# A block of attention and quantised FFN on one core: a normalisation's root begun by ScalarE, and context's split moved to the end of a step's first half

## Chip, cores and metric

The kernel runs on one NeuronCore of a Trainium2 chip. The metric is device time in microseconds, from a run of the program to its end. Lower is better.

## What is computed

The input x is 16 x 256 x 512 in fp32, the context has the same shape. The reference, cut to what matters:

```python
x = x + xattn(layernorm(x), ctx, ctx, wq, wk, wv, wo_w, wo_b)   # 16 heads of 32, rope, window 128
x = x + ffn(layernorm(x), W_in, b_in, W_out, b_out)             # 8-bit weights, 16-bit activations, gelu

def _layernorm(x, axis=-1, eps=1e-05):
    m = jnp.mean(x, axis=axis, keepdims=True)
    v = jnp.var(x, axis=axis, keepdims=True)
    return (x - m) / jnp.sqrt(v + eps)
```

The change concerns the first layernorm (its 1/sqrt(v + eps)), the order of work in the attention part, and one PSUM bank.

## The kernel before

The program is written engine by engine, each with its own instruction list in a fixed order; semaphores are the only coupling. Three parts follow each other: attention over 16 sequences (0 to some 760 us), the first FFN product, the second. Nothing in the second and third part is touched.

**The attention part** has a prologue and 16 steps, one for each sequence b. Step b does three things at a time: the scores, softmax and weighted sum of sequence b; the projections of sequence b + 1 (`has_proj`); the output product, residual and second normalisation's moments of sequence b - 1 (`has_o`). It also prepares sequence b + 2 (`has_xt`): its context is split, and the first normalisation's factors are found.

fp32 products are made of three fp32r products: each operand is split into a `_hi` (ScalarE, a cast) and a `_lo` (the difference, by VectorE or GpSimd).

A step has two halves.

- In the first half, TensorE makes the scores of 16 heads (`scores`, L605), and between them the tiles of b + 1: k (L521 to L523), the transpositions of x (`x_transposes`, L534), v, q. VectorE takes each head's row maxima (`row_maxima`, L1192), and between them `invert(b - 1)` (the reciprocal of the softmax sums, L1233), the rest of x, the rotations of k, and `normalise(b - 1)` (L1239).
- In the second half, TensorE makes the scores again, transposed (`scores_t`, L639), ScalarE their exponentials (`softmax_exp`, L961), GpSimd cuts them to the window (`band`, L1529), and TensorE multiplies them in four groups of four heads (`clump`: weighted sums L653, softmax sums L666). Among them stand the 24 products of `o_products` (L589) for b - 1, and before the last group `w_transposes` (L687), which needs a column block of W_in that VectorE has quantised.

**Around the change.**

- `ln1(j)` on VectorE: bn_stats and bn_aggr of two halves, then the root of v + eps by the bit trick and three Newton steps (`rsqrt_seed`, `rsqrt`, L285 to L293), then nmr = -mean x rstd. Seventeen linked instructions; each waits for the one before by the semaphore `ln1_chain`. `norm1(j)` on ScalarE applies it to x.
- `ctx_hi(j)` on ScalarE (L912, one cast of 128x1024) and `ctx_lo(j, quarter)` on GpSimd (L1512, four quarters of 128x256) split the context. `ctx_hi` waits for the load and for the v tiles of j - 1, which read the same buffer.
- `x_transposes(j, s)` writes half s to `q_bank[s]`, banks 4 and 5. Bank 5 also holds the softmax sums, so half 1 waits for `den_done`, the end of L1233.
- `oT_copy` (L931) brings the weighted sums out of banks 6 and 7; `centre` (L949) makes x minus its mean, whose largest magnitude VectorE then takes (`largest`, L1163).
- SyncE issues every transfer, in one order. In a step: load x for the residual of b - 1 (L325), store the reciprocals (`den_scratch`, L356), wait, load them back spread out (the "shares", L359), load x of b + 2, spread the maxima (L350), then the stackings of k and q of b + 1 (`stack_group`, L343; a group's first waits for `k_lo` or `q_lo`), the next block of W_in, the next context, more stackings, and the store of b - 1 (L329). The load L325 waits for that store. `normalise` needs the shares.

Of the kernel before, what the change touches and what calls it, by code (L numbers as in the profile page):

```python
# [29 lines left out]
P = 128  # L30
# [26 lines left out]
LN1_OPS = 17  # L57
# [28 lines left out]
def build(nc, t):  # L86
# [12 lines left out]
    with ExitStack() as ctx:  # L99
# [95 lines left out]
        pv_bank = bank[6:8]  # L195
        den_bank = q_bank[1]
# [8 lines left out]
        ln1_chain, ln1_norm = sem("ln1_chain"), sem("ln1_norm")  # L205
# [82 lines left out]
        def rsqrt(dve, link, v, r, tmp):  # L288

            for _ in range(3):  # L290
# [226 lines left out]
        def _(pe):  # L517
# [7 lines left out]
            def x_transposes(j, s):  # L525

                if s == 0:
                    pe.wait_ge(ln1_norm, 2 * j + 2)
                    wait(pe, wt_done, j - 1)
                    wait(pe, rope_step["q"], ROPE_OPS * j)  # L530
                else:
                    wait(pe, den_done, j - 1)
                for c in range(KC):
                    mm = pe.transpose(q_bank[s][:, c * P:(c + 1) * P], x_ln[:, s, c * P:(c + 1) * P], ident[:])  # L534
                mm.then_inc(xt_mm, 1)

            def v_tile(j, s, chunks=range(KC)):

                if chunks[0] == 0 and j == 1:
                    pe.wait_ge(v_done, s + 1)  # L540
                elif chunks[0] == 0:
                    wait(pe, oT_out, 2 * (j - 2) + s + 1)
                for c in chunks:
                    tok = slice(s * P, (s + 1) * P)
                    mm = split3(pv_bank[s][:], (cT_hi[:, c, tok], cT_lo[:, c, tok]),
                                (w_hi["wv"][:, c], w_lo["wv"][:, c]), c == 0, c == KC - 1)
                if chunks[-1] == KC - 1:
                    mm.then_inc(v_mm, 1)

            def qk_tile(j, which, half):  # L550

                src = (t_hi, t_lo) if which == "q" else (cT_hi, cT_lo)
                if which == "k":
                    if half == 0:
                        pe.wait_ge(c_hi, j + 1)
                        pe.wait_ge(c_lo, KC * (j + 1))
                    wait(pe, res_done, 2 * (j - 2) + half - 1)
                    if half == 0:
                        wait(pe, exp_done, H * (j - 1) - 2)
                    if j == 1:  # L560
                        pe.wait_ge(rope_step["k"], ROPE_OPS)
                elif half == 0:
                    pe.wait_ge(xt_hi, 2 * j + 2)
                    pe.wait_ge(xt_lo, 2 * j + 2)
                dst = (kv_bank if which == "k" else q_bank)[half]
                w = "w" + which
                for a in range(2):
                    e = slice((2 * half + a) * P, (2 * half + a + 1) * P)
                    for c in range(KC):
                        mm = split3(dst[:, a * S:(a + 1) * S], (w_hi[w][:, c, e], w_lo[w][:, c, e]),  # L570
                                    (src[0][:, c], src[1][:, c]), c == 0, c == KC - 1)
                mm.then_inc(qk_mm[which], 1)
# [328 lines left out]
        def _(act):  # L901
# [11 lines left out]

            def norm1(j):
# [8 lines left out]
            def xt_lead(j, s):  # L923
                act.wait_ge(xt_mm, 2 * j + s + 1)
                lead(q_bank, s, xt_hi)
# [53 lines left out]

            wk_hi(0)  # L980
# [14 lines left out]
            ctx_hi(1)  # L995

            def step(b, par, has_c, has_o, has_proj, has_xt):
# [10 lines left out]
                if has_proj:  # L1008
                    v_copy(b + 1, 1 - par, 1)
                max_copy(b, 0, slice(0, 2))  # L1010
                max_copy(b, 0, slice(2, KC))
                for n in range(H):
# [3 lines left out]
                    if n == 9 and has_xt:  # L1016
                        ctx_hi(b + 2)
                    if n in (8, 9, 10, 11) and not has_proj:
                        first_tile(n - 8)
                    if n == 12:  # L1020
                        oT_copy(b, 0)
                    if n == 13 and has_o:
                        centre(b - 1, 0)
                if has_o:
                    centre(b - 1, 1)
# [109 lines left out]
        def _(dve):  # L1135
# [6 lines left out]
            def ln1(j):  # L1142
# [3 lines left out]
                moments(link, x_ln, 0, 1)  # L1146
                wait(dve, ln1_norm, 2 * j)
                link(dve.tensor_scalar(veps[:], mv[:, 0, :, 1], EPS, None, ALU.add))
                rsqrt_seed(dve, link, veps[:], rstd[:])
                rsqrt(dve, link, veps[:], rstd[:], nt_t[:])  # L1150
                link(dve.scalar_tensor_tensor(out=nmr[:], in0=mv[:, 0, :, 0], scalar=-1.0, in1=rstd[:],
                                              op0=ALU.mult, op1=ALU.mult))
                assert link.count[0] == LN1_OPS
# [74 lines left out]
            def xt_rest(j, s):  # L1228
                rest(q_bank, s, xt_hi, 2 * j + s + 1, xt_lo)
# [27 lines left out]
            ln1(0)  # L1257
# [42 lines left out]
            ln1(1)  # L1300
            weight_lo(4, "wo")

            def step(b, par, has_c, has_o, has_proj, has_xt):
# [197 lines left out]
        def _(pool):  # L1501
# [35 lines left out]
            def step(b, par, has_c, has_o, has_proj, has_xt):  # L1537
# [5 lines left out]
                if has_o:  # L1543
                    ot_rest(b - 1, 0)
                    ot_rest(b - 1, 1)
                for n in range(H):
# [3 lines left out]
                    if 10 <= n < 14 and has_xt:  # L1550
                        ctx_lo(b + 2, n - 10)
# [53 lines left out]
```

## Time and profile before

| | before |
|---|---|
| median of 3 runs | 1230.52 us (1228.41 to 1232.91) |
| the profiled execution: its time, its span | 1230.85 us, 1228.3 us |
| TensorE busy | 1148.1 us, 93% of the span |
| VectorE busy | 979.9 us, 80% |
| ScalarE busy | 639.9 us, 52% |
| GpSimd busy | 361.2 us, 29% |
| mean granted clock of TensorE | 0.986 of full speed |
| chain that ended last | VectorE 37%, TensorE 35%, no visible wait 24% |

A busy share is an average over three different parts. In the profile PE is TensorE, DVE VectorE, ACT ScalarE, POOL GpSimd, and SPq the queue of SyncE. A name such as L1192 is the line of the kernel before. The steps are counted from 0; step 6 runs from about 303 to 347 us on TensorE.

### The profile page before, as it was taken

How to read it: one execution, taken by the hardware profiler on the slowest of the kernel's cores; microseconds unless marked ns; L12 is line 12 of the kernel's file. 1: busy time of each engine (PE TensorE's matmuls, PEld its weight loads, DVE VectorE, ACT ScalarE, POOL GpSimd, SP SyncE). 2: the span in 40 equal slices, each digit the busy share in tenths (PEclk: the TensorE clock that was granted, in tenths of full speed). 3: DMA queues.
4: the chain of work that ended last, by engine and by line, in shares of the span. 5: the costliest groups of instructions: out<-in, count | busy, mean ns of one | idle time of the engine just before them, and what ended most of it. 6: DMA issues, size and time to landing. Idle time of an engine off the chain costs nothing.

```text
span 1228.3 us, 23590 instructions
## 1 busy us (share of the span) xinstructions
PE 1148.1 (93%) x7884; PEld 767.8 (63%) x7928; DVE 979.9 (80%) x2541; ACT 639.9 (52%) x1001; POOL 361.2 (29%) x540
## 2 busy tenths in 40 slices
PE   6989999999999999999999867999999999999998
PEld 6857776877776777787677545444444444444443
DVE  6868989989899998998998746666666678777776
ACT  5254354345335435434533433655556568777774
POOL 1135336345444534634644331000000012111111
PEclk9989999999999999999999969999999999999999
DMA  8554664565565466456555532455554211667772
GB/s 269 127 135 109 170 175 118 152 176 138 142 177 149 110 173 165 113 164 171 146 139 145 143 121 77 144 204 199 204 206 175 95 60 35 187 219 239 237 223 94
DMA packets 100522, 191.10 MB, mean 156 GB/s; under 512 B 13376, under 2 KB 30912, under 8 KB 100416
## 3 DMA queue, kind: packets, MB, share of 16 engines
q1 hardware_dynamic: 100416, 189.75, 52.4%
q8 instruction: 59, 0.97, 0.3%
q14 instruction: 47, 0.39, 0.1%
HBM read 89.16 MB, written 43.91 MB: 108 GB/s over the span
## 4 chain that ended last, share of the span: by engine, by line
DVE 37%; PE 35%; issue 24%; DMA 2%; ACT 1%; SPq 1%; POOL 0%; DVEq 0%; POOLq 0%
PE bank L858 18%; DVE bank L1192 7%; PE bank L521 4%; PE bank L522 4%; PE bank L523 4%; DVE bn L1138 3%; DVE roped L1218 3%; DVE rt L1215 2%; DVE rt L1216 2%; DVE row_max L1192 2%; PE bank L605 2%; DVE neg_max L1233 2%; DVE x_res L1185 2%; DVE nt_t L292 2%; DVE nt_t L291 1%
## 5 line engine op out<-in xcount | busy, mean ns | idle before, releaser
L1192 DVE CUSTOM_DVE_ANT_0 bank<-bank,mask 128x256 f32<-128x256 f32 x512 | 201.8, 454 | 43.5 <-PE bank L605 36.6
L858 PE MATMUL bank<-wout_int,g_lo 128*128 128x512 bf16 x512 | 193.6, 379 | 1.1
L819 PE MATMUL bank<-qT_lo,win_int 128*128 128x512 bf16 x496 | 188.0, 379 | 1.2
L858 PE MATMUL bank<-wout_int,g_hi 128*128 128x512 bf16 x491 | 185.8, 379 | 0.3 <-issue 0.2
L819 PE MATMUL bank<-qT_hi,win_int 128*128 128x512 bf16 x474 | 179.6, 379 | 0.0
L961 ACT ACTIVATE probs<-bank 128x512 f32<-128x512 f32 x256 | 143.2, 604 | 36.8 <-PE bank L639 32.2
L1529 POOL TENSOR_SCALAR_AFFINE_SELECT probs<-probs 128x256 f32<-128x256 f32 x256 | 108.6, 427 | 80.4 <-ACT probs L961 74.3
L605 PE MATMUL bank<-k_st,q_st 96*128 96x256 f32 x512 | 98.8, 305 | 25.1 <-DVE row_max L1192 23.3
L1484 DVE TENSOR_TENSOR g_lo<-h_int,g_hi 128x512 f16<-128x512 f32 x128 | 89.1, 696 | 41.4 <-ACT g_hi L1101 37.8
L1522 POOL TENSOR_TENSOR x_res<-x_res,wo_b 128x512 f32<-128x512 f32 x32 | 43.4, 1375 | 253.8 <-DMA x_res<-in_x 246.5
L1069 ACT ACTIVATE h_ring<-bank,b_in,g_scale 128x512 f32<-128x512 f32 x96 | 73.0, 778 | 71.3 <-PE bank L819 54.8
L1426 DVE TENSOR_REDUCE hmax<-h_ring 128x512 f32 (+1 forms) x96 | 63.3, 683 | 58.3 <-ACT h_ring L1069 56.3
L639 PEld LDWEIGHTS bank<-q_st,k_st 128*128 128x128 f32 x512 | 90.4, 191 | 30.9 <-issue 13.6
L605 PEld LDWEIGHTS bank<-k_st,q_st 96*128 96x128 f32 x512 | 76.0, 194 | 51.0 <-DVE row_max L1192 36.9
L639 PE MATMUL bank<-q_st,k_st 128*128 128x256 f32 x512 | 103.7, 292 | 2.7 <-ACT probs L961 1.3
L1101 ACT CAST g_hi<-h_int 128x512 f16<-128x512 f32 x128 | 79.0, 617 | 47.3 <-PE bank L858 43.2
L1570 POOL TENSOR_TENSOR xq<-xq,b_out 128x512 f32<-128x512 f32 x32 | 41.2, 1288 | 166.8 <-ACT h_int L1110 166.8
L858 PEld LDWEIGHTS bank<-wout_int,g_hi 128*128 128x128 f16 x512 | 50.0, 98 | 60.9 <-issue 0.6
L858 PEld LDWEIGHTS bank<-wout_int,g_lo 128*128 128x128 f16 x512 | 50.1, 98 | 60.3 <-DVE g_lo L1484 0.2
L653 PE MATMUL bank<-probs,v_sb 128*32 128x256 f32 x1024 | 69.4, 389 | 16.4 <-POOL probs L1529 16.4
L819 PEld LDWEIGHTS bank<-qT_lo,win_int 128*128 128x128 bf16 x496 | 48.5, 98 | 57.8
L819 PEld LDWEIGHTS bank<-qT_hi,win_int 128*128 128x128 bf16 x496 | 48.5, 98 | 57.7
(170 smaller groups left out, 2725.5 us busy)
## 6 DMA issues: line engine op xcount, KB each, us to landing
hidden_scratch<-h_ring SPq DMA_DIRECT2D x96, 256.0 KB, 2.1
h_ring<-hidden_scratch SPq DMA_DIRECT2D x96, 256.0 KB, 2.8
k_st<-k_hi SPq DMA_DIRECT2D x128, 128.0 KB, 2.7
q_st<-q_hi SPq DMA_DIRECT2D x128, 128.0 KB, 2.6
xq<-x_scratch SPq DMA_DIRECT2D x16, 1024.0 KB, 5.9
x_ln<-in_x SPq DMA_DIRECT2D x16, 512.0 KB, 4.5
ctx_raw<-in_ctxT SPq DMA_DIRECT2D x16, 512.0 KB, 5.0
k_st<-k_lo SPq DMA_DIRECT2D x64, 128.0 KB, 2.7
```

Of the source, the lines that this page charges most:

```text
L605: mm = pe.matmul(ring[n % 2][:, qb * S:(qb + 1) * S], q_st[0:MROW, n, qb * P:(qb + 1) * P], k_st[0:MROW, n], start=True, stop=True)
L639: mm = pe.matmul(third[n][:, kb * S:(kb + 1) * S], k_st[:, n, kb * P:(kb + 1) * P], q_st[:, n], start=True, stop=True)
L653: mm = pe.matmul(pv_bank[i // 2][DK * c:DK * (c + 1), (i % 2) * S:(i % 2 + 1) * S], v_sb[:, par, kb, n], probs[:, n % SLOTS, kb], start=kb ...
L819: mm = pe.matmul(bank[f % 4][:], win_int[:, c, f * P:(f + 1) * P], part[:, par, c], start=c == 0 and part is qT_hi, stop=c == KC - 1 and p ...
L858: return pe.matmul(bank[4 * par + u][:], part[:, f % 4, u * P:(u + 1) * P], wout_int[:, f], start=f == 0 and part is g_hi, stop=f == FC - ...
L961: act.activation(probs[:, n % SLOTS].rearrange("p k q -> p (k q)"), third[n][:], ACT.Exp, scale=SCORE_SCALE).then_inc(exp_done, 1)
L1069: act.activation(dst, bank[f % 4][:], ACT.Gelu, bias=b_in[:, f:f + 1], scale=g_scale[:, f:f + 1]).then_inc(gelu_done, 1)
L1101: act.copy(g_hi[:, f % 4], h_int[:, f % 4]).then_inc(ghi_done, 1)
L1192: dve.tensor_tensor_reduce(sc, sc, mask[:, (1 - qb) * P:(1 - qb) * P + S], 1.0, NEG, ALU.add, ALU.max, row_max[:, qb, n:n + 1]).then_inc(m ...
L1426: dve.tensor_reduce(hmax[:, bass.ds(FC * n + f, 1)], src, AX_X, ALU.max, apply_absolute_value=True).then_inc(hmax_done, 1)
L1484: dve.tensor_tensor(g_lo[:, f % 4], h_int[:, f % 4], g_hi[:, f % 4], ALU.subtract).then_inc(glo_done, 1)
L1529: pool.affine_select(out=far, in_=far, compare_op=ALU.is_ge, fill=0.0, base=1 - P, pattern=[[0, 2], [1, P]], channel_multiplier=1).then_in ...
```

## The change

Four edits, all in the attention part.

1. `ln1` is cut in two. `ln1_stats` (the moments and v + eps) now stands before `quantise_win`, `ln1_finish` (one Newton step and nmr) behind it. The start value of the Newton step comes from ScalarE: `root1` takes a logarithm, then exp(-0.5 x log). The seed and two Newton steps are gone.
2. `ctx_hi(b + 2)` moves on ScalarE from behind exponential 9 to before the copy of the maxima (the end of the first half); on GpSimd two quarters of `ctx_lo` move ahead of band 0 and the others behind bands 1 and 3, from behind bands 10 to 13.
3. On ScalarE the first `oT_copy` and the first `centre` move from behind exponentials 12 and 13 to behind exponential 15.
4. Half 1 of the transposed x goes to bank 6 instead of bank 5. It waits for the `oT_copy` of bank 6 of the step before instead of `den_done`; that wait moves to the second q tile, and the v tile that uses bank 6 next waits for the rest of x.

```diff
-LN1_OPS = 17
+LN1_OPS = 9
+LN1_STATS = 5
+        x_bank = [bank[4], bank[6]]
@@ x_transposes, v_tile, qk_tile (TensorE)
+                elif j == 1:
+                    pe.wait_ge(v_done, 1)
                 else:
-                    wait(pe, den_done, j - 1)
+                    wait(pe, oT_out, 2 * j - 3)
                 for c in range(KC):
-                    mm = pe.transpose(q_bank[s][:, c * P:(c + 1) * P], x_ln[:, s, c * P:(c + 1) * P], ident[:])
+                    mm = pe.transpose(x_bank[s][:, c * P:(c + 1) * P], x_ln[:, s, c * P:(c + 1) * P], ident[:])
...
+                if s == 0:
+                    pe.wait_ge(xt_lo, 2 * j + 2)
...
+                else:
+                    wait(pe, den_done, j - 1)
@@ ScalarE
+            def root1(j):
+                act.wait_ge(ln1_chain, LN1_OPS * j + LN1_STATS)
+                act.activation(nt_t[:], veps[:], ACT.Ln).then_inc(ln1_root, 1)
+                act.wait_ge(ln1_root, 2 * j + 1)
+                act.activation(rstd[:], nt_t[:], ACT.Exp, scale=-0.5).then_inc(ln1_root, 1)
...
+            act.preload_act_table_set("natural_log_exp_and_others")
+            root1(0)
             wk_hi(0)
             ctx_hi(0)
...
             ctx_hi(1)
+            root1(1)
...
                 if has_proj:
                     v_copy(b + 1, 1 - par, 1)
+                if has_xt:
+                    ctx_hi(b + 2)
                 max_copy(b, 0, slice(0, 2))
                 max_copy(b, 0, slice(2, KC))
                 for n in range(H):
                     softmax_exp(b, n)
                     if n == 6 and has_proj:
                         split_hi("q", b + 1)
-                    if n == 9 and has_xt:
-                        ctx_hi(b + 2)
+                    if n == 10 and has_xt:
+                        root1(b + 2)
                     if n in (8, 9, 10, 11) and not has_proj:
                         first_tile(n - 8)
-                    if n == 12:
-                        oT_copy(b, 0)
-                    if n == 13 and has_o:
-                        centre(b - 1, 0)
+                oT_copy(b, 0)
                 if has_o:
+                    centre(b - 1, 0)
                     centre(b - 1, 1)
                 oT_copy(b, 1)
@@ VectorE
+            def ln1_finish(j):
+                dve.wait_ge(ln1_root, 2 * (j + 1))
                 wait(dve, ln1_norm, 2 * j)
-                link(dve.tensor_scalar(veps[:], mv[:, 0, :, 1], EPS, None, ALU.add))
-                rsqrt_seed(dve, link, veps[:], rstd[:])
-                rsqrt(dve, link, veps[:], rstd[:], nt_t[:])
+                link = chain(dve, ln1_chain, LN1_OPS * j + LN1_STATS)
+                rsqrt(dve, link, veps[:], rstd[:], nt_t[:], 1)
...
+                if has_xt:
+                    ln1_stats(b + 2)
                 quantise_win(b)
                 if has_xt:
-                    ln1(b + 2)
+                    ln1_finish(b + 2)
@@ GpSimd
                     ot_rest(b - 1, 0)
                     ot_rest(b - 1, 1)
+                if has_xt:
+                    ctx_lo(b + 2, 0)
+                    ctx_lo(b + 2, 1)
                 for n in range(H):
                     band(b, n)
                     if 6 <= n < 10 and has_proj:
                         split_lo("q", b + 1, n - 6)
-                    if 10 <= n < 14 and has_xt:
-                        ctx_lo(b + 2, n - 10)
+                    if n in (1, 3) and has_xt:
+                        ctx_lo(b + 2, n // 2 + 2)
```

TensorE's and SyncE's instructions keep their order; the other three change theirs. Three places follow. Line numbers of the changed kernel differ from those of before.

ScalarE, second half of step 1, before (exponentials are `probs<-bank`, `cT_hi` is context's cast, `oT` the copy of the sums, `rt` the centring):

```order
L942 COPY v_sb<-bank 128x512
L954 CAST q_st<-bank 32x512 x2
L961 ACTIVATE probs<-bank 128x512 x7
L907 CAST q_hi<-roped 128x1024
L961 ACTIVATE probs<-bank 128x512 x3
L912 CAST cT_hi<-ctx_raw 128x1024
L961 ACTIVATE probs<-bank 128x512 x3
L931 COPY oT<-bank 128x512
```

And now:

```order
L956 COPY v_sb<-bank 128x512
L920 CAST cT_hi<-ctx_raw 128x1024
L968 CAST q_st<-bank 32x512 x2
L975 ACTIVATE probs<-bank 128x512 x7
L915 CAST q_hi<-roped 128x1024
L975 ACTIVATE probs<-bank 128x512 x4
L924 ACTIVATE nt_t<-veps 128x2
L926 ACTIVATE rstd<-nt_t 128x2
L975 ACTIVATE probs<-bank 128x512 x5
L945 COPY oT<-bank 128x512
L963 ACTIVATE rt<-x_res,mv 128x512 x2
```

The cast is ahead of the maxima's copy, the root's two activations stand after exponential 10, and five exponentials now run without anything between them.

GpSimd, step 1, from x's bias on, before (`probs` are the bands):

```order
L1522 TENSOR_TENSOR x_res<-x_res,wo_b 128x512 x2
L1506 TENSOR_TENSOR k_lo<-roped,k_hi 128x256 x4
L1517 TENSOR_TENSOR t_lo<-oT,t_hi 128x4x128 x2
L1529 AFFINE_SELECT probs<-probs 128x256 x7
L1506 TENSOR_TENSOR q_lo<-roped,q_hi 128x256
L1529 AFFINE_SELECT probs<-probs 128x256
```

And now:

```order
L1547 TENSOR_TENSOR x_res<-x_res,wo_b 128x512 x2
L1531 TENSOR_TENSOR k_lo<-roped,k_hi 128x256 x4
L1542 TENSOR_TENSOR t_lo<-oT,t_hi 128x4x128 x2
L1537 TENSOR_TENSOR cT_lo<-ctx_raw,cT_hi 128x256 x2
L1554 AFFINE_SELECT probs<-probs 128x256 x2
L1537 TENSOR_TENSOR cT_lo<-ctx_raw,cT_hi 128x256
L1554 AFFINE_SELECT probs<-probs 128x256 x2
L1537 TENSOR_TENSOR cT_lo<-ctx_raw,cT_hi 128x256
L1554 AFFINE_SELECT probs<-probs 128x256 x3
```

Context's quarters stand before and between bands 0 to 4, and no longer between bands 10 and 14.

VectorE, second half of step 2, behind the quantisation of W_in, before (square brackets: semaphores waited for):

```order
L1252 COPY win_amax<-w_s 128x1 [waits wq_chain]
L1138 BN_STATS bn<-x_ln 128x6 [waits xln_in,wq_chain]
L1140 BN_AGGR mv<-bn 128x2 [waits ln1_chain]
L1138 BN_STATS bn<-x_ln 128x6 [waits ln1_chain]
L1140 BN_AGGR mv<-bn 128x2 [waits ln1_chain]
L1148 TENSOR_SCALAR veps<-mv 128x2 [waits ln1_norm,ln1_chain]
L285 TENSOR_SCALAR rstd<-veps 128x2 [waits ln1_chain]
L286 TENSOR_SCALAR rstd<-rstd 128x2 [waits ln1_chain]
L291 TENSOR_TENSOR nt_t<-rstd 128x2 [waits ln1_chain]
```

And now:

```order
L1273 COPY win_amax<-w_s 128x1 [waits wq_chain]
L293 TENSOR_TENSOR nt_t<-rstd 128x2 [waits ln1_norm,ln1_root,wq_chain]
L294 SCALAR_TENSOR_TENSOR nt_t<-nt_t,veps 128x2 [waits ln1_chain]
L295 SCALAR_TENSOR_TENSOR rstd<-nt_t,rstd 128x2 [waits ln1_chain]
L1172 SCALAR_TENSOR_TENSOR nmr<-mv,rstd 128x2 [waits ln1_chain]
L1206 TENSOR_TENSOR x_res<-bank,x_res 128x512 [waits o_mm,ln1_chain]
```

The moments have moved ahead of the quantisation, four instructions of the root are left, and the first of them waits for ScalarE (`ln1_root`).

## Rows read from the trace of the kernel before

**Rows 1.** Waits, 0 to 760 us: total us, times, longest.

```profile
PE bank L653 <- POOL probs L1529: 16.4, 16, 1.1
...
PE bank L534 <- DVE neg_max L1233: 6.7, 13, 0.5
```

**Rows 2.** Timeline of VectorE, steps 6 and 7: start us, us, instruction.

```profile
306.17 1.75 DVE L1233 RECIPROCAL neg_max<-bank 128x256 f32<-128x256 f32 x1
...
335.22 0.69 DVE L1245 TENSOR_REDUCE w_s<-w_raw 128x1 f32<-128x512 f32 x1
...
340.43 0.32 DVE L285 TENSOR_SCALAR rstd<-veps 128x2 int32<-128x2 int32 x1
...
345.76 0.69 DVE L1185 TENSOR_TENSOR x_res<-bank,x_res 128x512 f32<-128x512 f32 x1
...
348.94 0.42 DVE L1192 CUSTOM_DVE_ANT_0 bank<-bank,mask 128x256 f32<-128x256 f32 x1
...
350.43 1.75 DVE L1233 RECIPROCAL neg_max<-bank 128x256 f32<-128x256 f32 x1
```

**Rows 3.** Timeline of TensorE, same stretch; in brackets the idle time before.

```profile
343.88 0.40 PE L687 MATMUL bank<-ident_b,w_q 128*128 128x128 bf16 x4
345.38 1.07 PE L653 MATMUL bank<-probs,v_sb 128*32 128x256 f32 x16 [1.11 <-POOL probs L1529]
...
347.24 0.74 PE L605 MATMUL bank<-k_st,q_st 96*128 96x256 f32 x4
...
352.24 0.66 PE L534 MATMUL bank<-ident,x_ln 128*128 128x128 f32 x4 [0.51 <-DVE neg_max L1233]
```

**Rows 4.** Timeline of ScalarE, same stretch.

```profile
326.45 0.58 ACT L942 COPY v_sb<-bank 128x512 f32<-128x512 f32 x1
329.51 1.06 ACT L954 CAST q_st<-bank 32x512 fp32r<-32x512 f32 x2 [2.49 <-PE bank L617]
...
338.18 1.05 ACT L912 CAST cT_hi<-ctx_raw 128x1024 fp32r<-128x1024 f32 x1
...
342.98 1.09 ACT L961 ACTIVATE probs<-bank 128x512 f32<-128x512 f32 x2
```

**Rows 5.** Timeline of GpSimd, same stretch.

```profile
326.10 2.52 POOL L1517 TENSOR_TENSOR t_lo<-oT,t_hi 128x512 fp32r<-128x512 f32 x2 [1.28 <-ACT t_hi L938]
...
332.63 1.11 POOL L1529 TENSOR_SCALAR_AFFINE_SELECT probs<-probs 128x256 f32<-128x256 f32 x2 [0.28 <-ACT probs L961]
...
336.09 0.73 POOL L1506 TENSOR_TENSOR q_lo<-roped,q_hi 128x256 fp32r<-128x256 f32 x1 [0.15 <-ACT q_hi L907]
...
344.56 0.77 POOL L1529 TENSOR_SCALAR_AFFINE_SELECT probs<-probs 128x256 f32<-128x256 f32 x2
```

**Rows 6.** SyncE's waits over the run: total us, times, longest.

```profile
SPq L298 <- POOL q_lo L1506: 56.4, 15, 5.4
```

**Rows 7.** The load of the shares (L359): its own answer, over 15 steps.

```profile
DMA to landing us min/median/max: 3.5/3.8/5.1
```

**Rows 8.** Timeline of SyncE: that load in steps 6 and 9.

```profile
319.33 0.59 SPq L359 DMA_DIRECT2D probs<-den_scratch  x1
...
450.19 0.59 SPq L359 DMA_DIRECT2D probs<-den_scratch  x1
```

**Rows 9.** Timeline of VectorE: L1239, which needs the shares, steps 6, 9, 15.

```profile
323.30 2.07 DVE L1239 TENSOR_TENSOR oT<-oT,probs 128x512 f32<-128x512 f32 x2
...
455.39 1.50 DVE L1239 TENSOR_TENSOR oT<-oT,probs 128x512 f32<-128x512 f32 x2
...
719.18 1.29 DVE L1239 TENSOR_TENSOR oT<-oT,probs 128x512 f32<-128x512 f32 x2 [8.85 <-DMA probs<-den_scratch]
```

**Rows 10.** Timeline of TensorE in step 0.

```profile
43.51 0.50 PE L605 MATMUL bank<-k_st,q_st 96*128 96x256 f32 x2 [0.25 <-DVE row_max L1192]
44.28 0.51 PE L605 MATMUL bank<-k_st,q_st 96*128 96x256 f32 x2 [0.27 <-DVE row_max L1192]
```

**Rows 11.** Windows, step 0: us, busy of PE, PEld, DVE, ACT, POOL, clock, DMA share, GB/s.

```profile
67.80:74.60 6.80, 6.08 (x41) 3.54 (x42) 5.76 (x17) 3.87 (x7) 4.73 (x9) 0.52 0.70 165
```

More of the change, by code:

```diff
@@ L204, in build @@
         ctx_in, xln_in, xres_in, win_in, x1_out = (sem(n) for n in ("ctx_in", "xln_in", "xres_in", "win_in", "x1_out"))
-        ln1_chain, ln1_norm = sem("ln1_chain"), sem("ln1_norm")
+        ln1_chain, ln1_root, ln1_norm = sem("ln1_chain"), sem("ln1_root"), sem("ln1_norm")
         ln2_chain, y2_done, dmax_done = sem("ln2_chain"), sem("y2_done"), sem("dmax_done")
@@ L286, in rsqrt_seed, with rsqrt @@
             link(dve.tensor_scalar(r.bitcast(I32), r.bitcast(I32), -1.0, RSQRT_SEED, ALU.mult, ALU.add))
-        def rsqrt(dve, link, v, r, tmp):
-            for _ in range(3):
+        def rsqrt(dve, link, v, r, tmp, rounds=3):
+            for _ in range(rounds):
                 link(dve.tensor_tensor(tmp, r, r, ALU.mult))
@@ L924, in xt_lead @@
                 act.wait_ge(xt_mm, 2 * j + s + 1)
-                lead(q_bank, s, xt_hi)
+                lead(x_bank, s, xt_hi)
             def oT_copy(j, half):
@@ L1140, in moments, with ln1_stats @@
                 link(dve.bn_aggr(mv[:, which, s], bn[:, which, s]))
-            def ln1(j):
+            def ln1_stats(j):
                 dve.wait_ge(xln_in, 16 * (j + 1))
@@ L1146, in ln1 @@
                 moments(link, x_ln, 0, 1)
+                link(dve.tensor_scalar(veps[:], mv[:, 0, :, 1], EPS, None, ALU.add))
+                assert link.count[0] == LN1_STATS
+            def ln1_finish(j):
+                dve.wait_ge(ln1_root, 2 * (j + 1))
                 wait(dve, ln1_norm, 2 * j)
-                link(dve.tensor_scalar(veps[:], mv[:, 0, :, 1], EPS, None, ALU.add))
-                rsqrt_seed(dve, link, veps[:], rstd[:])
-                rsqrt(dve, link, veps[:], rstd[:], nt_t[:])
+                link = chain(dve, ln1_chain, LN1_OPS * j + LN1_STATS)
+                rsqrt(dve, link, veps[:], rstd[:], nt_t[:], 1)
                 link(dve.scalar_tensor_tensor(out=nmr[:], in0=mv[:, 0, :, 0], scalar=-1.0, in1=rstd[:],
                                               op0=ALU.mult, op1=ALU.mult))
-                assert link.count[0] == LN1_OPS
+                assert link.count[0] == LN1_OPS - LN1_STATS
             def ln2_moments(j, s):
@@ L1228, in xt_rest @@
             def xt_rest(j, s):
-                rest(q_bank, s, xt_hi, 2 * j + s + 1, xt_lo)
+                rest(x_bank, s, xt_hi, 2 * j + s + 1, xt_lo)
             def invert(b):
@@ L1256, in _ @@
             dve.memset(idle_b, 0.0).then_inc(idle_done, 1)
-            ln1(0)
+            ln1_stats(0)
+            ln1_finish(0)
             dve.memset(neg_max[:], 0.0).then_inc(const_done, 1)
@@ L1299, in _ @@
             dve.wait_ge(c_in, 16 * TABLES)
-            ln1(1)
+            ln1_stats(1)
+            ln1_finish(1)
             weight_lo(4, "wo")
```

## The prediction

> **What bounds the kernel now.** I read the page first: its busy shares, in the table above, give TensorE 93% of the span and VectorE 80%, so time can come only from what TensorE waits for. The list of waits for the attention part (0 to 760 us) has two that the edits touch [rows 1]. L653, the last head group's products, waits for GpSimd's bands (L1529), 16.4 us in 16 steps; the timeline puts 0.4 of it in the last step, so 1.07 in each of the others. L534, the second transposition of x, waits for the reciprocal L1233, 6.7 us in 13 steps, 0.52 each. The timelines of one step say why. On VectorE nothing is idle from 335.22 to 350.43: quantisation, the moments of x, the root and the residual run straight into the next step's row maxima, which start at 348.94 [rows 2], although TensorE issued their scores at 347.24 [rows 3]. The reciprocal stands behind the first two heads' maxima, so bank 5 comes free at 350.43 + 1.75 = 352.18, and TensorE resumes at 352.24 after 0.51 idle. On GpSimd four parts of context stand between the bands of heads 10 to 14, each about as long as the q_lo of the same shape, 0.73; the last two bands start only at 344.56 and end at 345.33 [rows 5], and TensorE resumes at 345.38 after 1.11 idle [rows 3].
>
> A step is then 350.43 - 306.17 = 44.3 us from one reciprocal to the next [rows 2], of which TensorE loses 1.6 to these two waits.
>
> **VectorE's part.** From 340.43 to 345.76 [rows 2] twelve small instructions take 5.3 us, 0.44 each with their links: two of the seed, nine of Newton's, one for nmr. Eight go (the seed and two Newton steps), 3.5 us; four stay, 1.8 us. So the second residual could start near 342.2, and VectorE reach the next row maxima at about 345.4. TensorE can't have scores ready before 346.1 (347.24 less the 1.11 that go). VectorE's late start of 1.7 us is gone, and TensorE doesn't wait for it there. But the row that matters is the transposition: it now goes to bank 6 and waits for a ScalarE copy of the step before instead of the reciprocal. Either of the two alone takes the 0.52 away; both together give it once: 13 x 0.52 = **6.7 us**.
>
> **ScalarE's part.** Logarithm and exponential on 128x2 have no row. Below they cost nothing, above what a 32x512 cast takes, 0.53 [rows 4]. I take 0.2 each, near VectorE's instructions of that shape (0.32 with their wait [rows 2]). They stand between exponentials 10 and 11; from context's cast, now 1.05 earlier in the order, they inherit the place at 338.18 to 339.2 [rows 4], so even 2 x 0.53 fits. The root's input is there: the moments go ahead of the quantisation, which starts at 335.22 [rows 2] and lasts half of the time up to 340.43, so they end near 337.8. The cast itself goes ahead of the maxima's copy: ScalarE is free from 326.45 + 0.58 = 327.03 and waits 2.49 there, until 329.51 [rows 4], so its 1.05 is covered; without that cover it would delay every exponential by up to 1.05. The copy of bank 6 and the centring leave the exponentials: the last two, which now end at 342.98 + 1.09 = 344.07, end about 343.1. VectorE's two maxima of the centred rows then end near 345.8, still ahead of the scores.
>
> **GpSimd's part.** Quarters 0 and 1 of context's parts run after t_lo, which ends at 326.10 + 2.52 = 328.62; two take 1.5, and the first band starts only at some 331.4 (332.63 less two bands of 0.45 and 0.28 idle [rows 5]): covered. Quarter 2 pushes bands 2 and 3 by at most 0.73, into 0.28 idle: they end near 334.1. Quarter 3 goes before band 4. Both are made up by 336.09, since q_lo waits there for ScalarE [rows 5]. With nothing between bands 10 and 15, the last follows its exponential: 343.1 + 0.45 = 343.6, before TensorE is through with L687 (343.88 + 0.40 [rows 3]). The 1.07 go in steps 0 to 13, **15.0 us**. Not in 14 and 15, where no context is split and what follows a step hangs on a transfer (below) or on the centring, whose end doesn't move.
>
> **The start.** The second root of the prologue gets 1.5 us shorter, and TensorE waits for row maxima 0.25 and 0.27 behind it [rows 10]: **0.5 us**.
>
> **What takes the place.** Nothing speeds up SyncE. Its queue starts each step's last row of stackings when q_lo is done (it waits for that 15 times, 56.4 us in all [rows 6]), then issues some twenty transfers, stores x1, loads x, stores the reciprocals and loads the shares, which L1239 of the next step needs. Against q_lo all of TensorE's savings bring L1239 forward, the transfers not. The slack is L1239's start minus (issue + landing). Step 6: 323.30 - (319.33 + 3.8) = 0.2; step 9, with the longest landing, 455.39 - (450.19 + 5.1) = 0.1 [rows 7 to 9]. Read so, steps 2 to 14 have 1.8, 1.8, 2.6, 1.8, 0.2, 1.2, 1.7, 0.1, 2.7, 1.5, 1.4, 2.3, 3.4, in all 22.3. A step can win at most the smaller of 1.59 and its slack, so steps 6, 7, 9, 11 and 12 give back 1.4 + 0.4 + 1.5 + 0.1 + 0.2 = **3.6 us**. Step 15 already waits 8.85 for its shares [rows 9]; there every gain after q_lo of step 14 is lost.
>
> **The sum.** 15.0 + 6.7 + 0.5 - 3.6 = 18.6 us. The profiled execution took 1230.85 us (span 1228.3), 0.3 above the median of the three runs: 1230.85 - 18.6 = **1212 us**.
>
> **A rule weighed.** GpSimd's quarters move from beside VectorE's small instructions to beside the rotation of q and the first quantisation. L1239 took 2.07 for its two where it ran beside GpSimd, and 1.29 in step 15 [rows 9], so one neighbour costs up to 0.4 an instruction. The sum has nothing for it, since q_hi waits for exponential 6, not for the rotation. The Trainium skill (SBUF — State Buffer, section Who interferes with whom) says that a VectorE instruction with two SBUF inputs and a GpSimd instruction that reads SBUF exclude each other for their whole length. By that rule the extra 0.78 in L1239 is what one would expect, and each moved quarter could block or be blocked once.
>
> **The rivals.**
> 1. *The shares bind harder.* Four quarters pushed by 0.4 each on GpSimd, the two late ones ahead of q_lo: q_lo 0.7 later, every slack 0.7 smaller. Then steps 2 to 14 win 11.3 instead of 17.0: 13 us, 1218. Against it, the 0.15 that q_lo waits for ScalarE shows only that the two meet.
> 2. *A mutual block each time.* If each quarter waits out a two-input instruction of 0.69, the two late quarters move q_lo by 1.4; steps 2 to 14 win 3.7, the sum is 5.3: 1225.5. This is what the skill's rule gives at its worst; no row of context's quarters shows it, since they never ran there.
> 3. *ScalarE becomes late.* If root, copy and centring hold the last copy of a step, or exponentials 11 to 15, the wait of L653 stays and only 7 us go: 1223.5.
> 4. *Slower.* The shares come more than 1.8 us later against q_lo. Steps 2 to 14 then change by 22.3 - 13x, with 1.6 of the rest: zero at x = 1.8, and at x = 2.5 it is 8.6 slower, 1239.5. It takes a GpSimd queue that runs over its cover before q_lo, or landings like step 9's 5.1 in most steps. A reload of ScalarE's tables at each root would do it too, but the instruction list has none between the roots.
> 5. *More is won.* Landings move in time and the slacks of steps 6 and 9 were chance; VectorE's head start also shortens its waits at the end of the first half. 3.6 comes back and some 4 us more: 1204.
>
> **Chances.** Forecast (1207 to 1216) 0.57; rival 1 0.15; rival 2 0.06; rival 3 0.06; rival 4 0.06; rival 5 0.10. The range for 8 in 10 reaches from rival 5 into rivals 1 and 3: 1204 to 1223. In step 0 TensorE's granted clock was 0.52 over 6.8 us [rows 11], the lower level, 1.2 GHz; a spell more or less is some 3 us either way and lies within it. A measurement tells 0.3%, 3.7 us, from no change. Faster 0.87 (all but rival 4 and a part of 2 and 3), same 0.07, slower 0.06.
>
> **What will show it.** L653's wait for GpSimd near zero until step 13; no wait of the second transposition, nor any for the new copy; the last band's start about 1 us earlier against L687; a new wait of L1239 for the shares in some of steps 2 to 14, under 1.5 us each; a step of 42.7 us. I am wrong if q_lo comes later against L687, if ScalarE's exponentials 11 to 15 wait for the root, or if the sum of L1239's waits passes 10 us before step 15.

## The result: slower by 1.3%

| | before | changed |
|---|---|---|
| median | 1231.10 us (4 runs) | 1245.97 us (4 runs, 1244.34 to 1250.74) |
| ratio | 1 | 1.0129, 95% interval 1.0093 to 1.0165 |
| span of the profiled execution | 1228.3 us | 1242.7 us |
| mean granted clock of TensorE | 0.986 | 0.962 |
| TensorE busy | 1148.1 us | 1166.3 us |

The forecast was 1212 us with a range of 1204 to 1223, and 6 in 100 for slower. The two waits that it counted on did go, as it said. The time did not.

The list of waits of the kernel before, 0 to 760 us (total us, times, longest), where [rows 1] has its other two:

```profile
PE bank L605 <- DVE row_max L1192: 23.3, 41, 10.1
...
PE bank L617 <- DVE neg_max L1199: 7.6, 15, 2.1
```

And of the changed kernel:

```profile
PE bank L613 <- DVE row_max L1213: 38.6, 37, 10.5
...
DVE oT L1260 <- DMA probs<-den_scratch: 18.1, 8, 9.2
PE bank L625 <- DVE neg_max L1220: 16.6, 15, 2.7
```

L661 (L653 of before) waits for GpSimd nowhere, nor L538 (L534) for the reciprocal: 16.4 + 6.7 = 23.1 us are gone. But the scores of the last heads wait for row maxima 38.6 us, 23.3 before, and the transposition of the maxima (L625, L617 of before) waits for neg_max 16.6 us, 7.6 before. The four waits came to 54.0 us before and come to 55.2 now. What TensorE waits for at these places was not removed. It was gathered at the end of each first half. And its busy time grew by 18.2 us for the same matmuls, where the span grew by 14.4. (The trace of before has 7884 matmul records, that of the changed kernel all 7928; at the mean length the missing ones are some 6 us, so the growth lies between 12 and 18.)

**Where the busy time comes from.** Four windows of the changed kernel (us, then busy time and instructions of PE, PEld, DVE, ACT, POOL, granted clock, DMA share, GB/s):

```profile
280.90:287.70 6.80, 6.09 (x20) 5.21 (x21) 5.13 (x8) 2.85 (x5) 2.61 (x5) 0.51 0.26 60
325.30:332.10 6.80, 5.97 (x17) 4.43 (x18) 6.38 (x21) 3.09 (x6) 3.88 (x4) 0.51 0.01 2
373.00:379.90 6.90, 6.00 (x19) 4.52 (x19) 5.87 (x12) 2.26 (x5) 2.88 (x5) 0.51 0.25 57
147.80:151.20 3.40, 3.10 (x10) 2.67 (x11) 3.33 (x6) 1.29 (x3) 0.90 (x2) 0.52 0.11 27
```

At the end of the first half of 11 of steps 1 to 14 the granted clock falls to its lower level, 1.2 GHz, for 3.4 to 6.8 us. The kernel before has no such spell in steps 1 to 14. The stretch from 75 to 685 us, before and then changed:

```profile
75.00:685.00 610.00, 573.47 (x4860) 460.36 (x4859) 548.62 (x1614) 276.92 (x471) 281.94 (x443) 1.00 0.56 148
75.00:685.00 610.00, 573.38 (x4734) 466.01 (x4734) 500.15 (x1458) 269.65 (x479) 269.51 (x421) 0.95 0.55 146
```

The mean clock is 0.95 for 1.00 over 610 us: some 30 us at full speed not granted, of which TensorE's busy time shows 12 to 18.

**Where the idle time comes from.** The end of step 5's first half, VectorE (start us, us, instruction):

```profile
274.78 2.11 DVE L1260 TENSOR_TENSOR oT<-oT,probs 128x512 f32<-128x512 f32 x2
...
280.09 0.77 DVE L1218 TENSOR_SCALAR neg_max<-row_max 128x32 fp32r<-128x32 f32 x1
280.90 0.66 DVE L1220 SCALAR_TENSOR_TENSOR neg_max<-row_max,neg_max 128x32 fp32r<-128x32 f32 x1
```

GpSimd and TensorE at the same moment:

```profile
277.62 2.52 POOL L1542 TENSOR_TENSOR t_lo<-oT,t_hi 128x512 fp32r<-128x512 f32 x2 [1.28 <-ACT t_hi L952]
280.11 1.39 POOL L1537 TENSOR_TENSOR cT_lo<-ctx_raw,cT_hi 128x256 fp32r<-128x256 f32 x2
```

```profile
277.73 0.50 PE L613 MATMUL bank<-k_st,q_st 96*128 96x256 f32 x2 [0.85 <-DVE row_max L1213]
278.49 0.50 PE L613 MATMUL bank<-k_st,q_st 96*128 96x256 f32 x2 [0.26 <-DVE row_max L1213]
...
281.61 0.69 PE L625 MATMUL bank<-ident,neg_max 128*128 128x128 f32 x2 [1.45 <-DVE neg_max L1220]
```

Context's first quarter starts at 280.11, 0.02 us after the first of two tiny instructions that stand between the last row maximum and everything in the second half. They take 0.77 and 0.66 us, and the second ends at 281.56, 0.06 after the two quarters. In the kernel before they took 180 to 183 and 191 to 194 ns in all 16 steps. Their own answers now:

```profile
L1218 DVE TENSOR_SCALAR neg_max<-row_max x16: 181/604/772, 60.2 to 739.1; 128x32 fp32r<-128x32 f32 x16
...
L1220 DVE SCALAR_TENSOR_TENSOR neg_max<-row_max,neg_max x16: 191/656/658, 60.5 to 739.3; 128x32 fp32r<-128x32 f32 x16
```

TensorE waits 1.45 us for them here and 0.56 to 1.45 in steps 1 to 13, 0.4 before. The meeting is no accident of one step: t_lo waits for a ScalarE cast of what L1260 writes, and the last row maxima follow L1260 on VectorE, so that both engines come to this point from the same instruction, and in steps 1 to 13, step 6 excepted, the quarter starts within 0.03 us of L1218. In other steps the shares come late as well: step 6 shows it on VectorE.

```profile
322.43 2.30 DVE L1260 TENSOR_TENSOR oT<-oT,probs 128x512 f32<-128x512 f32 x2 [1.50 <-DMA probs<-den_scratch]
```

L1260 also took longer, 29.4 us in all for its 30 instructions, 23.6 before (1020 and 828 ns in the mean). In step 5 it runs beside GpSimd's k_lo (273.07 to 276.34). So the rows account for what L613 and L625 wait more, 15.3 + 9.0 us: 9 us of late shares in steps 1 to 14, 6 of a longer L1260, and 9 behind neg_max. No run changes the second of these alone.

So four explanations lay open: late shares (A), context's parts at that place (B, and in its precise form D, the collision at neg_max), a clock that falls because TensorE has fewer pauses elsewhere (C), and the bank.

### The profile page after: what moved, and what is told of

It is laid out like the page before. It is cut to its first block, busy times and chain, and to the rows that moved or that the text cites. A ratio compares the mean times of both kernels' runs of the same rounds, so it can differ in the third digit from the quotient of the medians.

```text
span 1242.7 us, 23555 instructions
## 1 busy us (share of the span) xinstructions
PE 1166.3 (94%) x7928; PEld 785.9 (63%) x7928; DVE 945.2 (76%) x2413; ACT 644.7 (52%) x1033; POOL 364.3 (29%) x540
## 4 chain that ended last, share of the span: by engine, by line
PE 50%; issue 22%; DMA 9%; SPq 9%; DVE 9%; ACT 1%; POOL 0%; POOLq 0%; DVEq 0%; ACTq 0%
PE bank L866 18%; SPq L345 7%; PE bank L597 7%; PE bank L647 5%; PE bank L661 4%; DVE bank L1213 3%; PE bank L523 3%; PE bank L524 3%; PE bank L525 3%; PE bank L674 3%; DMA den_scratch<-neg_max 3%; DMA x_scratch<-x_res 3%; DMA probs<-den_scratch 2%; PE bank L613 2%; DVE oT L1260 1%
## 5 line engine op out<-in xcount | busy, mean ns | idle before, releaser
L866 PE MATMUL bank<-wout_int,g_hi 128*128 128x512 bf16 x512 | 193.7, 379 | 0.1
L827 PE MATMUL bank<-qT_hi,win_int 128*128 128x512 bf16 x496 | 188.1, 379 | 0.0
L975 ACT ACTIVATE probs<-bank 128x512 f32<-128x512 f32 x256 | 140.1, 600 | 61.2 <-PE bank L647 58.5
L613 PE MATMUL bank<-k_st,q_st 96*128 96x256 f32 x512 | 98.5, 305 | 39.9 <-DVE row_max L1213 38.6
L647 PEld LDWEIGHTS bank<-q_st,k_st 128*128 128x128 f32 x512 | 99.6, 208 | 31.2 <-issue 13.2
L613 PEld LDWEIGHTS bank<-k_st,q_st 96*128 96x128 f32 x512 | 76.4, 195 | 64.6 <-DVE row_max L1213 51.2
L647 PE MATMUL bank<-q_st,k_st 128*128 128x256 f32 x512 | 109.7, 306 | 2.0 <-ACT probs L975 1.1
L1127 ACT ACTIVATE h_int<-h_ring,magic_c,tiny 128x512 f32<-128x512 f32 x96 | 77.9, 812 | 0.0
```

The lines of the kernel that those rows point to most:

```text
L613: mm = pe.matmul(ring[n % 2][:, qb * S:(qb + 1) * S], q_st[0:MROW, n, qb * P:(qb + 1) * P], k_st[0:MROW, n], start=True, stop=True)
L647: mm = pe.matmul(third[n][:, kb * S:(kb + 1) * S], k_st[:, n, kb * P:(kb + 1) * P], q_st[:, n], start=True, stop=True)
L827: mm = pe.matmul(bank[f % 4][:], win_int[:, c, f * P:(f + 1) * P], part[:, par, c], start=c == 0 and part is qT_hi, stop=c == KC - 1 and p ...
L866: return pe.matmul(bank[4 * par + u][:], part[:, f % 4, u * P:(u + 1) * P], wout_int[:, f], start=f == 0 and part is g_hi, stop=f == FC - ...
L975: act.activation(probs[:, n % SLOTS].rearrange("p k q -> p (k q)"), third[n][:], ACT.Exp, scale=SCORE_SCALE).then_inc(exp_done, 1)
L1127: act.activation(h_int[:, f % 4], chunk, ACT.Identity, bias=magic_c[:], scale=tiny[:, 5:6]).then_inc(hint_done, 1)
```

## The experiments

Each was timed in alternation with the kernel before. Ratios are to that kernel, with the 95% interval.

| kernel | median us | ratio | mean clock, profiled run | L613 + L625 wait, us | shares wait, us |
|---|---|---|---|---|---|
| changed | 1245.97 | 1.0129 (1.0093 to 1.0165) | 0.962 | 38.6 + 16.6 | 18.1 |
| e1 shares first | 1247.51 | 1.0139 (1.0113 to 1.0165) | 0.962 | 34.7 + 5.2 | 8.8 |
| e2 fill | 1230.68 | 1.0007 (0.9986 to 1.0028) | 0.979 | 21.7 + 18.0 | 17.3 |
| e3 bank undone | 1243.05 | 1.0121 (1.008 to 1.0162) | 0.965 | 39.5 + 15.2 | 17.0 |
| e4 context undone | 1222.45 | 0.993 (0.9903 to 0.9958) | 0.980 | 27.6 + 7.2 | 10.2 |
| e5 quarters wait | 1222.46 | 0.9907 (0.9885 to 0.9929) | 0.969 | 40.9 + 4.4 | 17.8 |
| e6 context only | 1245.21 | 1.0098 (1.0069 to 1.0128) | 0.964 | 32.4 + 17.1 | 12.4 |
| e7 quarters wait, reciprocals first | 1212.23 | 0.9844 (0.98 to 0.9888) | 0.977 | 28.3 + 6.4 | 7.9 |
| e8 reciprocals first | 1230.52 | 0.9979 (0.9958 to 1.0001) | 0.967 | 30.4 + 15.4 | 11.0 |
| e9 bank only | 1224.22 | 0.9945 (0.9928 to 0.9962) | 0.983 | 26.6 + 7.1 | 11.0 |
| e10 root only | 1222.43 | 0.9928 (0.9908 to 0.9947) | 0.980 | 25.7 + 7.2 | 10.2 |
| e11 context undone, reciprocals first | 1220.43 | 0.9916 (0.9883 to 0.9949) | 0.986 | 24.0 + 7.5 | 9.7 |
| e12 as e7, with fill | 1208.04 | 0.9807 (0.9774 to 0.984) | 0.986 | 20.4 + 7.5 | 9.6 |

The last three columns are from the profiled execution, the last two of them from its list of waits. In e3, e4, e5 and e8 that execution lies 3 to 6 us off the median; the other executions of e5 had clocks of 0.971 to 0.975. Some 8 to 11 us of the share wait, and 9 to 13 of L613's, belong to step 15 in every kernel, before too.

### First round: what is it not?

**e1, the shares first.**

```diff
                 if has_o:
-                    load_xres(b - 1)
                     spread_shares(b - 1)
+                    load_xres(b - 1)
```

> The changed kernel, with one edit on SyncE: the reciprocals are stored and the shares loaded ahead of the load of x for the residual, which waits for the store of x1. Three theories. Late shares (A): removing TensorE's two waits brought VectorE's L1260 up against the transfer of the shares, the idle time gathers before the last heads' scores (3.2 us in step 5), and the granted clock falls there in 11 of 14 steps. Then the shares come 3 to 4 us sooner, no step from 1 to 14 waits for them, the idle time before the last scores is again 1 to 2 us, the low spells of steps 1 to 14 mostly go, and the time is 1210 to 1222. Position (B): context's parts on GpSimd and ScalarE disturb VectorE at the end of the first half. Then the waits for the shares go but the idle time and low spells stay: 1235 to 1242. Load (C): the clock falls because TensorE has fewer pauses elsewhere, whatever it waits for here. Then the low spells stay or grow: 1232 to 1245.

Measured: 1247.51 us, no gain. The waits for the shares went, as said (18.1 to 8.8, all of it in step 15). But x now lands later, and GpSimd's chain with it: bias, k_lo, t_lo. The output products wait for t_lo. TensorE in step 5:

```profile
284.20 0.50 PE L613 MATMUL bank<-k_st,q_st 96*128 96x256 f32 x2 [1.68 <-DVE row_max L1213]
...
286.65 0.77 PE L597 MATMUL bank<-wo_hi,t_hi 128*128 128x512 f32 x1 [1.18 <-issue]
```

That second wait is 18.4 us in 15 steps, and the changed kernel has none of it. The profile names no releaser (`issue`); the first of t_lo's two instructions ends at 286.54, 0.11 us ahead. Nor did the pair for neg_max stay as it was: t_lo, two instructions of 1.26 us each, now runs beside it (it starts at 285.29).

```profile
286.56 1.26 DVE L1218 TENSOR_SCALAR neg_max<-row_max 128x32 fp32r<-128x32 f32 x1
```

It ends with t_lo, and takes up to 1.28 in other steps. The edit moved one late transfer against another. It tells nothing against A by itself, so A was tried again with an edit that delays x less (e7, e8).

**e2, fill.** Sixteen idle matmuls before head 14's scores:

```diff
                     tiles[6] += [lambda: v_tile(b + 1, 1, range(2, KC))]
+                    if has_xt:
+                        tiles[6] += [lambda: fill(b)]
...
+            def fill(b):
+                pe.wait_ge(rope_step["k"], ROPE_OPS * (b + 2))
+                keep_busy(kv_bank[0], 16)
```

> The changed kernel, with 16 idle matmuls (128x256, bf16, into bank 2, as the prologue has them; some 1.8 us) put between the last v tile and the scores of head 14, in steps 0 to 13. They do no useful work and can only delay TensorE where its wait was shorter. A (idle time brings the clock down): the low spells of steps 1 to 13 go, which is worth some 27 us less what the fill costs in steps with a short wait (up to 0.8 each): 1218 to 1230. B: as A for the clock. C (load, not idleness): low spells stay or grow, 1245 or more.

Measured: 1230.68 us, 15 us less, with more work, the same waits for the shares and the same collision (L625 18.0). Only idle time was replaced by idle work. The clock between 75 and 685 us is 0.99 for 0.95; three short spells of steps 1 to 14 stay, of 3.5 us each. So the clock falls because TensorE is idle there, and the fall costs about what the whole change loses. C is out. The time lies just above the expected 1218 to 1230.

**e3, the bank undone.** Half 1 of x in bank 5 again (`x_bank = [bank[4], bank[5]]`, with its old waits).

> The changed kernel, with half 1 of the transposed x back in bank 5 behind the reciprocal. All theories: with VectorE early the wait for the reciprocal should stay small. A: nearly nothing changes, since VectorE's head start alone hides the reciprocal: 1240 to 1248, low spells as in the changed kernel. If the bank edit were what does the harm, it would be near 1225.

Measured: 1243.05 us, inside 1240 to 1248. The bank is not the cause.

**e4, context undone.** The cast behind exponential 9 and the quarters behind bands 10 to 13.

> The changed kernel, with context's cast and its four quarters back behind exponential 9 and bands 10 to 13. A: L653 waits for GpSimd again, TensorE reaches the next step 1 us later, the shares are late in fewer steps, and low spells are fewer: 1222 to 1234. B: VectorE's rotation and the bands are undisturbed again, the stall before the last scores is as before the change whatever the shares do: 1215 to 1224.

Measured: 1222.45 us, 23 us less than the changed kernel, although L661's wait for GpSimd is back (17.5 us in 14 steps). L625 waits 7.2 us again and the neg_max pair takes 181 and 193 ns in the mean. Without context's move there is no harm, and the root, the bank and the copies together are worth 8 us against the kernel before. The time lies at the joint of what A and B expected, so the run does not separate them; what separates them is e5.

### Second round: which part of context's move?

**e5, the quarters wait for neg_max.**

```diff
                 if has_xt:
+                    pool.wait_ge(msplit, 2 * (b + 1))
                     ctx_lo(b + 2, 0)
                     ctx_lo(b + 2, 1)
```

> The changed kernel, with one wait on GpSimd: quarters 0 and 1 of context's parts start only when VectorE has written both columns of neg_max. Collision (D): VectorE's two small instructions for neg_max (128x32) stand between the last row maximum and TensorE's transposition of the maxima. They took 0.18 and 0.19 us in every step of before, 0.50 and 0.58 in the mean in the changed kernel, where quarter 0 runs at that moment, and 0.18 and 0.19 again with context's move undone. Then here they take 0.18 and 0.19, TensorE's wait before that transposition falls from 0.8 to 1.5 back to 0.4, most low spells of steps 1 to 14 go, and the time is 1212 to 1224. Late shares (A) alone: the waits of L1260 for the shares and most low spells stay: 1238 to 1246.

Measured: 1222.46 us; one wait on GpSimd is worth 23 us. VectorE in step 5:

```profile
277.75 0.18 DVE L1218 TENSOR_SCALAR neg_max<-row_max 128x32 fp32r<-128x32 f32 x1
277.97 0.19 DVE L1220 SCALAR_TENSOR_TENSOR neg_max<-row_max,neg_max 128x32 fp32r<-128x32 f32 x1
```

and GpSimd:

```profile
278.24 1.42 POOL L1537 TENSOR_TENSOR cT_lo<-ctx_raw,cT_hi 128x256 fp32r<-128x256 f32 x2 [0.43 <-DVE neg_max L1220]
281.77 0.74 POOL L1554 TENSOR_SCALAR_AFFINE_SELECT probs<-probs 128x256 f32<-128x256 f32 x1 [2.12 <-ACT probs L975]
```

The quarters start 0.43 us behind t_lo, still in cover (2.12 idle before the first band), and the pair is back at 0.18 and 0.19. D is shown. Its second half was only half right: the low spells became short, some 3.5 us each, but did not go: there are 12 in steps 1 to 14, for 11 in the changed kernel. The waits for the shares stayed too (17.8), and e7 shows that they are part of the reason.

**e6, context's move alone** on the kernel before.

> The kernel before, with context's move alone (the cast on ScalarE and the four quarters on GpSimd). D: the wait of L653 for GpSimd goes (15 us), but both neg_max instructions take 0.5 to 0.7, TensorE idles 1 us more before the maxima's transposition in each step (14 us), and the clock falls there in some steps, so that it is slower than before: 1236 to 1250. If the harm needs the head start of VectorE and the shares (A), the clock stays and the time is 1218 to 1230.

Measured: 1245.21 us, 1.0% slower. The collision needs neither the new root nor VectorE's head start. L653's wait fell from 16.4 to 6.4 us, not to zero, probably because the copy and centring still stand among the exponentials (their move was not run alone); L617's rose from 7.6 to 17.1, L605's from 23.3 to 32.4, and L534's 6.7 went. That is 55.9 us for 54.0, the same waits in sum, and the clock at 0.96 between 75 and 685 us.

**e7 and e8, the reciprocals first.** SyncE stores the reciprocals, then loads x, then waits for the store and loads the shares. e7 has the edit of e5 too.

```diff
                 if has_o:
+                    store_den(b - 1)
                     load_xres(b - 1)
                     spread_shares(b - 1)
```

> As the kernel in which the quarters wait for neg_max, and SyncE also stores the reciprocals before it loads x for the residual, so that their landing runs beside the landing of x1; the shares can then be loaded some 4 us sooner and x comes 0.5 us later. D and A together: the waits of L1260 for the shares in steps 1 to 14 go (some 4 to 9 us, with the idle time that they make): 1206 to 1218, 3 to 8 below the kernel without it. If the shares never mattered, it equals that kernel within 3.

> The changed kernel, with the reciprocals stored first, as above, and the quarters as in the change. A: the waits of L1260 for the shares go, 9 us, and with them low spells: 1222 to 1234. D: the waits go, but the collision at neg_max and most low spells stay: 1236 to 1245.

Measured: e7 1212.23 us, e8 1230.52. Against the kernels without the edit that is 10 us (e5) and 15 us (the changed kernel). In both the waits for the shares shrink to step 15 and little else (7.9 and 11.0). So A is true as well, beside D: 10 to 15 us for late shares (15 is clear of the intervals, at 10 they touch), 18 (e8 to e7) to 23 (changed to e5) for the collision. In e8 the time is in A's range, but the low spells mostly stay, as D said: nine in steps 1 to 14, 42 us in sum for 63. In e7 five are left, of some 3.5 us, and in four steps the pair still meets t_lo (0.59 to 1.27 us). Taking away one of the two does not bring the forecast 1212; what they share is that both add idle time at one place, and in the table the clock goes with L613 + L625: 0.962 to 0.969 where their waits are 45 us or more, 0.977 and above where they are under 40. The exception is e1, 39.9 us and 0.962, which has its 18.4 us for t_lo directly behind.

### Third round: the other edits, and a better kernel

**e9 and e10, the bank alone and the root alone**, each on the kernel before, with its lines of the change.

> The kernel before with the bank edit alone. By the prediction's own term it takes away the 0.51 us wait behind the reciprocal in 13 steps, 6.7 us: 1223 to 1227, and nothing else moves. If the time saved there is given back at the shares (steps 6 and 9 have 0.1 to 0.2 us of slack), 1226 to 1230.

> The kernel before with the root alone (logarithm and exponential on ScalarE, one Newton step, the moments ahead of the quantisation); bank, context and copies as before. VectorE reaches the next maxima 1 to 2 us earlier, so the reciprocal is out of the way of bank 5: the same 0.51 us in 13 steps go, and 0.5 of the prologue: 1222 to 1227. If ScalarE's two instructions among the exponentials cost something, L653's wait grows from 1.1 and it is 1228 to 1234.

Measured: 1224.22 and 1222.43 us, both inside their first ranges, with L534's wait gone in either. Each gives some 6 to 8 us, and e4, which has both and the moved copies, 1222.45: together they give it once. ScalarE's price is in the changed kernel's rows: 203 to 215 ns for the logarithm, 203 for the exponential.

**e11, context undone, reciprocals first.**

> The changed kernel with context's parts back among the late bands, and the reciprocals stored ahead of the load of x. L653's wait for GpSimd stays (17 us), neg_max is undisturbed, the shares come early: nothing to wait for at the end of the first half but what was there before. If the shares bound that kernel in some steps, 1216 to 1221; if not, 1222. Against the kernel with waiting quarters and early reciprocals (1212) it says what context's move is worth once it is placed aside: 5 to 9 us, less than the 15 of its wait.

Measured: 1220.43 us, against 1222.45 without the edit of SyncE. The intervals overlap, so whether that part is worth anything there is open. Against e7 context's move, put aside from neg_max, is worth some 8 us, though e7's runs spread from 1208.36 to 1218.51 and the two intervals touch.

**e12, e7 with a fill of eight.**

> The kernel with waiting quarters and early reciprocals, with 8 idle matmuls (0.9 us) between the last v tile and the scores of head 14. It idles there 0.6 to 1.2 us in each step, and its clock still falls for 3.4 us in five steps. If idleness alone brings the clock down, these spells go and are worth 8 us, less 0.2 a step where the fill is longer than the wait: 1204 to 1212. If they come from the work around it, nothing is won: 1212 to 1218.

Measured: 1208.04 us, ratio 0.9807, the best of all. The clock of e12 over that part, where the changed kernel had 0.95:

```profile
75.00:685.00 610.00, 591.67 (x5090) 477.85 (x5088) 519.38 (x1540) 285.72 (x508) 295.32 (x449) 1.00 0.57 153
```

In e7 it was 0.99. Where e7 has five low spells in steps 1 to 14, e12 has one. The time is 4 us below e7's, less than the 8 expected, but the intervals of the two overlap (0.9774 to 0.984, 0.98 to 0.9888) and they were not timed against each other: that the fill pays here is likely, not shown. In e2 it is shown.

## Why the prediction was wrong

- **The two waits.** Right: 15.0 + 6.7 us were forecast, 16.4 + 6.7 went, L653's in steps 14 and 15 as well. Each is real: e9, e10 and e4 keep the 6.7, and e7 to e11 show context's at 8 when it stands aside.
- **GpSimd's part: the step that failed.** The prediction put the first two quarters behind t_lo at 328.62 and called them covered, since the first band starts only at 331.4 [rows 5]. That was cover for GpSimd. It asked what waits for the quarters, and not what VectorE does in that moment: L1197 and L1199, 0.18 and 0.19, at the hinge on which TensorE already waited. They took 0.60 and 0.66 in the median, and this cost 9.0 us of waits at L625 and, with the clock, 18 to 23 us. The trace of before had the place: in step 6 L1197 starts 0.05 us before t_lo ends at 328.62, the very moment that the text gives to quarter 0.

```profile
328.57 0.18 DVE L1197 TENSOR_SCALAR neg_max<-row_max 128x32 fp32r<-128x32 f32 x1
```

- **The rule weighed.** It was weighed at the wrong instruction. The prediction took the rotation of q and the first quantisation, and wrote that the sum has nothing for it, since q_hi waits for exponential 6. Its rival 2 had no row of context's quarters for a block, since they never ran at the new place. At the old one they ran beside the twelve small instructions, which the text took at 0.44 each, their mean. VectorE and GpSimd in step 6 of before:

```profile
343.96 0.66 DVE L293 SCALAR_TENSOR_TENSOR rstd<-nt_t,rstd 128x2 f32<-128x2 f32 x1
...
345.37 0.16 DVE L293 SCALAR_TENSOR_TENSOR rstd<-nt_t,rstd 128x2 f32<-128x2 f32 x1
```

```profile
343.88 0.72 POOL L1512 TENSOR_TENSOR cT_lo<-ctx_raw,cT_hi 128x256 fp32r<-128x256 f32 x1
```

The same instruction on 128x2 takes 0.66 behind a quarter and 0.16 behind the last band. The rule of the Trainium skill (SBUF — State Buffer, Who interferes with whom) says more than was used: what blocks is decided by who issues first, for the whole length. The trace agrees for L1220: where it starts 0.19 to 0.21 us behind quarter 0 (steps 1 to 3 and 9) it takes 0.59 or 0.60 and ends just after that quarter. It agrees for L1218 in steps 6 and 12, where the quarter starts first. In the other steps the records are too close to tell: L1218 starts 0.00 to 0.03 us before the quarter where it takes 0.18 and where it takes 0.77.
- **The shares.** Right as a mechanism and too small. The term was 3.6 us, under 1.5 in a step; the waits of steps 1 to 14 came to 18.1 - 9.2 = 8.9 us in 7 steps, the longest 2.72. L1260 itself, which the sum leaves as it was, took 5.8 us more. Earlier shares were worth 10 to 15 us with the clock.
- **The clock.** The prediction priced it at one spell, some 3 us either way, and held that time can come only from what TensorE waits for. The spells were 12 to 18 us of busy time, and 15 us by e2. Step 0 already held the sign [rows 11]: a low clock after waits of 2.07 and 0.67 us at 64.96 and 66.06. The text did not ask what idle time at one place may cost there. This is a little under half of the error of 34 us. The rest is the idle time that came back: 55.2 against 54.0 us, with which the result would have been no change.
- **The root, ScalarE.** As said. The start's 0.5 us were not looked at alone. The root's two instructions took 0.21 and 0.20; the forecast took 0.2. Nothing waited for them but VectorE, 3.3 us in 5 steps, off the path.
- **The rivals and the signs.** The fourth, slower, took a queue on GpSimd before q_lo or long landings. What happened was none of the five: a collision at the hinge, and the clock behind it. None of the three signs of being wrong came either: q_lo ended 3.3 to 3.5 us ahead of the transpositions of L687 in the steps looked at (2, 5 to 8, 10, 11), 3.5 before; the exponentials behind the root waited for TensorE's scores; and the waits for the shares stayed under 10 us. But a step took 45.5 us in the mean of steps 1 to 13, 43.9 before, where 42.7 was forecast. e7 comes out at 1212.23, but that it meets 1212 is in part luck: it has an edit of SyncE that takes away what the 3.6 stood for, and it keeps five low spells and 3.8 us more of waits at L613 and L625 than before.

What is not settled: how the 23 us of the collision divide between its direct idle time (12 us at L625, from the two lists of waits) and the clock, since each changes the other; and why the clock fell in one step and not in another. In the changed kernel TensorE's waits around the last scores and L625 came to 2.47 us in step 4, where it fell, and to 2.48 in step 11, where it did not.

## What to carry to other kernels

Work moved on GpSimd into its own idle time is not free: list what VectorE does in the same microsecond, the smallest instructions first, since a 0.18 us instruction that a whole engine waits for became 0.77 here, and 1.26 beside a longer neighbour. Look for the same pair in the trace of before: instructions of one line that take 0.16 in one place and 0.66 in another name the price. Removing a wait of TensorE moves its idle time to the next late thing; if several short pauses become one long one, look at the granted clock before and after, not only at the sum of idle time. Where such a pause can't be removed, idle matmuls in it kept the clock up and were worth 15 us here.

## What was not expected of the hardware

- In these runs the clock's fall follows idle time gathered at one place, not the total. The kernel before idled 54.0 us at the four places and had a mean clock of 1.00 from 75 to 685 us; the changed one idled 55.2 and had 0.95. At the end of the first half that was 0.65 to 1.46 us a step in steps 1 to 14 before, with no fall, and 1.97 to 4.25 us in the 11 steps with a fall, never more than 2.89 at a stretch.
- Filling that pause with 128x256 bf16 matmuls that do nothing brought it from 0.95 to 0.99, and the whole kernel from 1245.97 to 1230.68 us.
- Two VectorE instructions on 128x32 took 181 and 193 ns (median) in every step of the kernel before, where at most the last 0.05 us of a GpSimd instruction lay beside them, and up to 772 and 658 ns beside a two-input GpSimd instruction of 0.7 us, up to 1.28 and 1.22 us beside one of 1.26 (e1). One of them is a tensor_scalar with a single input tensor.
